# Modulation rows computed once, sent through DRAM and broadcast back, in a two-layer AdaLN attention and expert kernel

## The chip, the core and the metric

The kernel runs on one core of a Trainium2 chip. The metric is the device time of one execution in microseconds (us). The core has a matrix engine (TensorE, PE in the profile; PEld is its weight load), a vector engine (DVE), a scalar engine (ACT), a general engine (POOL) and a queue engine (SP), which here only issues DMAs. They run side by side and wait for each other on semaphores.

## The reference, cut to what matters

The input is x, 16 batches of 256 tokens of 128 features. Two layers follow each other. In each, six vectors per batch are made from a small table c (16 x 128) and a matrix wmod (128 x 768):

```python
mod = (silu(c) @ wmod).reshape(16, 6, 1, 128)
sa, ca, ga, sb, cb, gb = (mod[:, 0], mod[:, 1], mod[:, 2], mod[:, 3], mod[:, 4], mod[:, 5])
```

(sa, ca) shift and scale the normalised input of the attention, and (sb, cb) that of the second block; ga and gb are turned into gates that scale what a block adds to x. Layer 0 has a causal attention of 8 heads with a window of 128, then a second attention of 16 causal heads with a mixture of 8 experts behind it. Layer 1 has a full attention of 16 heads and a routed expert network. All of it is float32.

The kernel forms a gate from a vector g as sign times a clipped size, (g >= 0 ? 0.5 : -0.5) * 2 * max(0.25, |g|), and uses a scale as 1 + c.

## The kernel before

There are three attention stages, called here stage 0 (8 heads, layer 0), stage 1 (16 heads, layer 0) and stage 2 (16 heads, layer 1). The dense expert part lies between stages 1 and 2, the routed one after stage 2. Each stage walks through the 16 batches in a software pipeline. While the heads of batch b are multiplied (function `segment`), the head maxima of batch b+1 are found, the input of batch b+2 is prepared (`prep`), and the output of batch b-1 is finished (`post`). `start` prepares batches 0 and 1 of a stage; the other 14 batches are prepared inside segments.

The order is written out by hand. `order(c)` lists the steps of a segment, and `slots` spreads them over the heads, each step before or behind the value product of its slot. All five engines walk the same table, each taking from a step what is its own, and each engine works strictly in that order. A step on PE writes one of two PSUM banks, `ps_work` or the fourth bank of `ps_four`; `bank_of` gives them out in turn by the step's place among the steps that use PE.

The modulation rows are made anew for each batch and stage, 48 times, in two steps.

- In "stat", DVE copies the batch's column of silu(c) over 128 columns (`c_bcast`, L1449).
- In "mod", PE multiplies it with the wanted columns of wmod (L1665; 128, 384 or 512 columns in stages 0, 1 and 2), which gives the row in all 128 partitions. ACT copies it to `mod` in SBUF (L1290). DVE turns the gate parts into gates by four operations for each part (L1459, L1460, L1464, L1473). POOL adds 1 to the scale part (L1173) in stages 1 and 2.

DVE's next steps stand behind this. "xhat" (L1478) normalises the two token blocks of the batch, and "ht" (PE, L1676) transposes them. DVE also takes the head maxima (L1588 in stages 0 and 1, L1595 in stage 2), for which PE's maximum products (L1767) wait before they reuse one of two PSUM banks.

Lines that the prediction speaks of: `max_scores` L1767 and `exp_scores` L1803 on PE, `pair_values` L1834, "combine" L1725, "rstat" on DVE from L1547, ACT's cast of the selection matrices L1280, PE's small products in the prologue L982, y times the gate L1533, and the loading of the expert weights on SP's queue (`sp_tail`, tile wd).

## Time and profile before

| | us |
|---|---|
| median of 3 runs | 2430.91 |
| lowest and highest | 2418.29, 2470.23 |
| profiled execution, its own time | 2441.24 |
| its span | 2439.4 |
| PE busy (share of the span) | 2040.3 (84%) |
| DVE busy | 1150.1 (47%) |
| ACT busy | 738.2 (30%) |
| POOL busy | 404.9 (17%) |
| mean granted clock of TensorE | 0.713 |

In the rows below a time stamp is us from the start of the span, and L with a number is a line of the kernel. The granted clock is 1.00 at 2.4 GHz and 0.50 at 1.2 GHz, and a value between is a mean over a stretch. A float32 product shows as more than one record ("x2" for one product with 128 stationary columns). In the profile the stages lie at about 22 to 498 (stage 0), 498 to 1300 (stage 1) and 1610 to 2300 us (stage 2). The chain of work that ended last consists of PE to 75%, of DVE to 11%, and of POOL and of unexplained issue time to 5% each.

### The profile page before, as it was taken

The page shows a single profiled execution, that of the slowest core. Times are in us where ns is not written, and L with a number is a line of the kernel's source. Part 1 is how long each engine was busy: PE and PEld are TensorE (multiplying, and loading weights), DVE is VectorE, ACT ScalarE, POOL GpSimd, SP SyncE. Part 2 cuts the span into 40 slices and gives each one's busy share as a digit, 9 for nine tenths or more (in the row PEclk, how much of TensorE's full clock was granted, in tenths as well). Part 3 has the DMA queues.
Part 4 walks back from the last instruction along what each step waited for, and adds up shares of the span by engine and source line. Part 5 has one row for each costly group of instructions (what it writes and reads, how often), then busy time and mean ns, then how long its engine had stood idle before and what let it go on. Part 6 is the DMA issues. An engine that isn't in the chain of part 4 may idle for free.

```text
span 2439.4 us, 35232 instructions
## 1 busy us (share of the span) xinstructions
PE 2040.3 (84%) x11152; PEld 1325.0 (54%) x11152; DVE 1150.1 (47%) x4250; ACT 738.2 (30%) x1580; POOL 404.9 (17%) x643
## 2 busy tenths in 40 slices
PE   5888888968999999899997999968888888898390
PEld 3555555535555555555556888844554555454160
DVE  3454444345344434443426888845544445544202
ACT  1232333213332232233332222213434243434130
POOL 1111111022111211121100000021222122111505
PEclk9887787656555555555557999966878588858595
DMA  6000000000000000000000000010000000000132
GB/s 206 1 1 1 0 0 1 1 0 1 1 1 2 1 1 2 1 1 1 1 1 1 1 0 0 1 35 1 1 1 0 0 0 0 0 1 1 46 105 73
DMA packets 26201, 30.08 MB, mean 12 GB/s; under 512 B 3745, under 2 KB 19393, under 8 KB 25665
## 3 DMA queue, kind: packets, MB, share of 16 engines
q1 hardware_dynamic: 24000, 24.08, 3.1%
q0 software_dynamic: 2048, 4.20, 0.6%
q8 instruction: 68, 1.11, 0.2%
q14 instruction: 85, 0.69, 0.1%
HBM read 19.88 MB, written 8.39 MB: 12 GB/s over the span
## 4 chain that ended last, share of the span: by engine, by line
PE 75%; DVE 11%; POOL 5%; issue 5%; ACT 3%; DMA 1%; SPq 0%; DVEq 0%; POOLq 0%; ACTq 0%
PE ps_out L1834 15%; PE ps_max L1767 8%; PE ps_work L1725 5%; PE ps_four L1803 5%; PE ps_four L1007 5%; PE ps_max L1018 5%; PE ps_four L1681 4%; PE ps_work L1706 3%; PE ps_four L1706 3%; PE ps_four L1686 3%; PE ps_work L1665 2%; PE ps_four L1789 2%; DVE row_max L1595 1%; PE ps_max L1074 1%; DVE ps_max L1588 1%
## 5 line engine op out<-in xcount | busy, mean ns | idle before, releaser
L1401 ACT ACTIVATE attn_f<-ps_four 128x384 f32<-128x384 f32 (+1 forms) x640 | 339.1, 531 | 464.0 <-PE ps_four L1803 463.1
L1834 PE MATMUL ps_out<-attn_f,v_all 128*9 128x256 f32 (+3 forms) x2560 | 418.7, 468 | 0.6 <-ACT attn_f L1391 0.3
L1767 PE MATMUL ps_max<-k_st,q_st 24*128 24x256 f32 (+3 forms) x1280 | 333.9, 417 | 86.4 <-DVE row_max L1595 73.2
L1803 PE MATMUL ps_four<-q_st,k_st 26*128 26x256 f32 (+3 forms) x1280 | 388.2, 392 | 0.0
L1767 PEld LDWEIGHTS ps_max<-k_st,q_st 24*128 24x128 f32 (+1 forms) x1280 | 210.0, 254 | 213.2 <-issue 93.8
L1803 PEld LDWEIGHTS ps_four<-q_st,k_st 26*128 26x128 f32 (+1 forms) x1280 | 262.8, 252 | 31.2 <-issue 21.0
L1588 DVE CUSTOM_DVE_ANT_0 ps_max<-ps_max,q_masks 128x128 f32<-128x128 f32 (+1 forms) x768 | 256.1, 377 | 0.0
L1834 PEld LDWEIGHTS ps_out<-attn_f,v_all 128*9 128x9 f32 (+1 forms) x2560 | 118.4, 108 | 202.6 <-issue 151.6
L1595 DVE TENSOR_REDUCE row_max<-ps_max 128x2 f32<-128x512 f32 x256 | 168.7, 684 | 80.4 <-PE ps_max L1767 79.4
L1789 PE MATMUL ps_four<-masks,ident_bf 128*128 128x128 bf16 x384 | 106.6, 278 | 76.7 <-DVE row_max L1588 59.9
L1725 PEld LDWEIGHTS ps_work<-strips,attn_f 128*128 128x128 f32 x640 | 137.9, 324 | 16.4 <-issue 16.2
L1018 PEld LDWEIGHTS ps_max<-wd,o_both 128*128 128x128 f32 x1024 | 135.0, 193 | 18.3 <-DVE o_both L914 8.0
L1725 PE MATMUL ps_work<-strips,attn_f 128*128 128x36 f32 (+1 forms) x640 | 140.0, 399 | 2.3 <-ACT attn_f L1391 2.3
L1018 PE MATMUL ps_max<-wd,o_both 128*128 128x128 f32 x1024 | 137.1, 277 | 5.7 <-DVE o_both L914 5.5
L1789 PEld LDWEIGHTS ps_four<-masks,ident_bf 128*128 128x128 bf16 x384 | 47.4, 123 | 163.5 <-DVE row_max L1588 59.2
L1581 DVE COPY wait_cell<-one 128x1 f32<-128x1 f32 x384 | 57.1, 149 | 162.4 <-PE ps_max L1767 155.1
L1198 POOL TENSOR_TENSOR split<-rope_ab 128x256 fp32r<-128x256 f32 (+1 forms) x80 | 57.9, 723 | 426.1 <-DVE rope_ab L1504 426.1
L1007 PE MATMUL ps_four<-select,q_st 128*128 128x512 f32 x352 | 119.0, 419 | 1.6 <-DVE select L866 1.6
L1164 POOL TENSOR_TENSOR var_eps<-mean_var,eps 128x2 f32<-128x2 f32 x48 | 9.4, 196 | 646.5 <-DVE mean_var L1452 646.5
L1706 PE MATMUL ps_work<-split,select 128*128 128x256 f32 (+1 forms) x448 | 109.8, 381 | 2.4 <-ACT k_st L1332 2.3
L1791 PE MATMUL ps_four<-masks,ident_bf 128*128 128x128 bf16 x384 | 109.9, 286 | 0.0
L1588 DVE DVE_READ_ACCUMULATOR2_ANT row_max<- 128x1 f32 x768 | 108.0, 141 | 0.0
(243 smaller groups left out, 3069.5 us busy)
## 6 DMA issues: line engine op xcount, KB each, us to landing
wd<-in_L_ffn_W SPq DMA_DIRECT2D x16, 256.0 KB, 2.7
gates_all<-in_select SPq DMA_DIRECT2D x3, 1024.0 KB, 7.3
x_all<-in_L_attn_x SPq DMA_DIRECT2D x8, 256.0 KB, 6.9
slots_dram<-attn_f SPq DMA_DIRECT2D x8, 256.0 KB, 5.5
h_tok<-slots_dram SPq DMA_DIRECT2D x8, 256.0 KB, 2.8
y_dram<-o_both SPq DMA_DIRECT2D x8, 256.0 KB, 2.5
out_x<-x_all SPq DMA_DIRECT2D x16, 128.0 KB
wgu<-in_L_ffn_Wg SPq DMA_DIRECT2D x1, 1024.0 KB, 5.9
```

Source lines behind the costliest of these rows:

```text
L1007: last = nc.tensor.matmul(pairs[pair_of[u]][i], w, x, start=(j == 0), stop=(j == 2))
L1018: last = nc.tensor.matmul(ps_max[:, e % 2, k * D:(k + 1) * D], act_t[:, f, k * P:(k + 1) * P], wd[:, e, f, :], start=(f == 0 and k == 0), ...
L1401: nc.scalar.activation(probs[:, h % 4, 0:w], ps_exp[:, h % 3, 0:w], ACT.Exp, scale=c.scale).then_inc(exp_done, 1)
L1588: ins = nc.vector.tensor_tensor_reduce(ps_max[:, i % 2, first:last], ps_max[:, i % 2, first:last], q_masks[:].rearrange("p n m -> p (n m)" ...
L1595: nc.vector.tensor_reduce(row_max[:, r2, :, h], src, AX_X, ALU.max).then_inc(max_done, 1)
L1706: last = nc.tensor.matmul(bank[:, g * S:(g + 1) * S], select[0:rows, 2 * i + part, 2 * (j % 2) + g, :], split[0:rows, i, part, :], start=( ...
L1725: last = nc.tensor.matmul(columns[:, k, g, i], o_strips[:, g, at:at + P], strips[:, c.kind, 1:1 + w], start=True, stop=True)
L1767: ins = nc.tensor.matmul(bank[:, at:at + keys.stop], q_st[rows, r, g, k * P:(k + 1) * P], k_st[rows, r, g, keys], start=True, stop=True)
L1789: nc.tensor.matmul(bank[:, 0:P], ident_bf[:], masks[:, 0, :], start=True, stop=False, skip_group_check=True)
L1791: nc.tensor.matmul(bank[:, S:S + P], ident_bf[:], masks[:, 0, :], start=False, stop=False, skip_group_check=True)
L1803: ins = nc.tensor.matmul(bank[:, k * S:(k + 1) * S - first], k_st[rows, r, g, k * P:(k + 1) * P], q_st[rows, r, g, first:S], start=not c.c ...
L1834: last = nc.tensor.matmul(ps_out[base:base + c.hd + 1, at + first:at + S], v_tok[c.index][:, r, kb, h // (c.heads // c.kv), :], probs[:, h ...
```

## The change

The rows are computed once for all batches in the prologue. With silu(c) as stationary operand (16 columns) PE multiplies it with four of the six parts of wmod for each layer, ga, sb, cb and gb. ACT copies the result, 16 partitions by 1024, into `mod_rows`. DVE adds 1 to the scales and forms the gates on it at the end of the start of stage 0 (`mod_gates`). SP stores this to a DRAM tensor `mod_dram` and loads the parts that a batch needs, with a broadcast over the 128 partitions, into the ring `mod` of four batches, ahead of time and in the order of the batches; the gates gb of a layer come in one load for all batches. The step "mod" is gone on all engines, and the copy to `c_bcast` with it. In its place "stat" has a tiny copy of eps. DVE waits for the load of a batch's rows where it first uses them, at y in stages 0 and 2 and behind xhat in stage 1. The selection matrices of the next stage are loaded by SP between those loads, as the diff shows.

With one step less the table of slots shifts: almost every step lies half a head or one head earlier, and the two PSUM banks swap roles.

```diff
@@ the table of steps @@
-            return (["stat", "mod", "xhat"] + (["sq", "hn"] if c.index == 1 else []) + ["ht", "combine", "q", "ot"]
+            return (["stat", "xhat"] + (["sq", "hn"] if c.index == 1 else []) + ["ht", "combine", "q", "ot"]
@@ ACT, prologue @@
+            act.wait_ge(pro_pe, 4)
+            nc.scalar.copy(mod_rows.rearrange("b l k d -> b l (k d)"), ps_four[0:NB, 0:2, :]
+                           ).then_inc(mod_rows_out, 1)
@@ DVE, expert part and end @@
+                dve.wait_ge(gates_load, 16)
...
+            dve.wait_ge(gates_load, 32)
@@ PE, prologue @@
+            for layer in range(2):
+                last = nc.tensor.matmul(ps_four[0:NB, layer, :], silu_c[:, layer, :], wmod[:, layer, 2 * D:],
+                                        start=True, stop=True)
+            last.then_inc(pro_pe, 1)
@@ SP @@
+            def load_mod(c, b, r):
+                n = n_of(c, b)
+                if c.index == 1 and not isinstance(b, int):
+                    sp.wait_ge(h_done, b - RING + 1)
+                elif c.index == 2 and not isinstance(b, int):
+                    sp.wait_ge(rt_h, b - RING + 1)
+                elif c.index < 2 and not (c.index == 0 and isinstance(b, int)):
+                    sp.wait_ge(y_out, n - RING + 1)
+                lo, hi = c.parts
+                sp.dma_start(mod[:, r, 0:hi - lo, :],
+                             mod_dram[c.layer, bass.ds(b, 1), lo:hi, :].rearrange("o k d -> (o k) d").partition_broadcast(P)
+                             ).then_inc(mod_load[r], 16)
...
+            sp.wait_ge(mod_rows_dve, 3)
+            sp.dma_start(mod_dram.rearrange("l b k d -> b l k d"), mod_rows).then_inc(mod_store, 16)
+            sp.wait_ge(mod_store, 16)
+            for r in range(RING):
+                load_mod(CFGS[0], r, r)
+            load_select(1)
+            load_later_mods(CFGS[0])
+            for r in range(RING):
+                load_mod(CFGS[1], r, r)
+            load_gates(0)
+            load_later_mods(CFGS[1])
+            sp.wait_ge(moe_done, NB // 2)
+            load_select(2)
+            for r in range(RING):
+                load_mod(CFGS[2], r, r)
+            load_gates(1)
+            load_later_mods(CFGS[2])
             sp_tail(sp)
@@ POOL @@
-                if name == "mod" and c.index > 0:
-                    pool.wait_ge(mod_out, n + 1)
-                    scale = mod[:, r, c.index, :]
-                    nc.gpsimd.tensor_tensor(scale, scale, one[:].to_broadcast([P, D]), ALU.add).then_inc(mod_scale, 1)
@@ ACT @@
-                if name == "mod":
-                    act.wait_ge(mod_mm, n + 1)
-                    at_least(act, y_out, n - RING + 1)
...
-                    nc.scalar.copy(mod[:, r, 0:c.parts, :].rearrange("p a d -> p (a d)"),
-                                   work[bank_of(c, name)][:, 0:c.parts * D]).then_inc(mod_out, 1)
@@ DVE @@
-                    nc.vector.tensor_copy(c_bcast[:, r2, :], silu_c[:, c.layer, bass.ds(b, 1)].to_broadcast([P, P])
-                                          ).then_inc(c_bcast_done, 1)
+                    nc.vector.tensor_copy(var_eps[:, r2, :], eps[:])
...
-                if name == "mod":
-                    dve.wait_ge(mod_out, n + 1)
...
-                        dve.wait_ge(mod_scale, n - NB + 1)
+                        dve.wait_ge(mod_load[r], 4 * (n - r) + 16)
...
+                        dve.wait_ge(mod_load[r], 4 * (n - r) + 16)
                         nc.vector.tensor_tensor(y_tok[:, r2], y, mod[:, r, 0:1, :].to_broadcast([P, BLK, D]),
@@ DVE, called at the end of the start of stage 0 @@
+            def mod_gates():
+                gates = [mod_rows[:, layer, 0::3, :] for layer in range(2)]
+                dve.wait_ge(mod_rows_out, 1)
+                nc.vector.tensor_scalar(mod_rows[:, :, 2, :], mod_rows[:, :, 2, :], 1.0, None, ALU.add)
+                for layer in range(2):
+                    nc.vector.tensor_scalar(gate_rows[:, 0, layer], gates[layer], 0.0, 0.5, ALU.is_ge, ALU.subtract)
+                    last = nc.vector.scalar_tensor_tensor(gate_rows[:, 1, layer], gates[layer], -1.0, gates[layer],
+                                                          ALU.mult, ALU.max)
...
@@ PE @@
-                if name == "mod":
-                    pe.wait_ge(c_bcast_done, n + 1)
-                    nc.tensor.matmul(bank[:, 0:c.parts * D], c_bcast[:, r2, :],
-                                     wmod[:, c.layer, c.mod:c.mod + c.parts * D],
-                                     start=True, stop=True).then_inc(mod_mm, 1)
```

The order moves at three places that matter. The first is PE in the loop of stage 2, from the value product of head slot 1 on (ps_max and ps_four are the maximum and the score products of a head, ps_out the value product). Before:

```order
L1834 MATMUL ps_out<-attn_f,v_all 9x256 x4
L1664 REGISTER_ALU
L1665 MATMUL ps_work<-wmod,c_bcast 128x512
L520 REGISTER_ALU x2
L1767 MATMUL ps_max<-k_st,q_st 128x256
L1803 MATMUL ps_four<-q_st,k_st 128x256
...
L520 REGISTER_ALU
L1676 MATMUL ps_four<-ident,h_tok 128x128 x2
L1824 REGISTER_ALU
L520 ISA
L1834 MATMUL ps_out<-attn_f,v_all 9x256 x4
L1725 MATMUL ps_work<-strips,attn_f 128x36 x8
```

and of the change:

```order
L1857 MATMUL ps_out<-attn_f,v_all 9x256 x4
L517 REGISTER_ALU x2
L1790 MATMUL ps_max<-k_st,q_st 128x256
L1826 MATMUL ps_four<-q_st,k_st 128x256
...
L1699 MATMUL ps_work<-ident,h_tok 128x128 x2
L517 REGISTER_ALU x2
L1803 REGISTER_ALU
...
L1740 ISA
L1748 MATMUL ps_four<-strips,attn_f 128x36 x8
L1847 REGISTER_ALU
L1857 MATMUL ps_out<-attn_f,v_all 9x256 x4
```

The product of 512 columns is gone, the transposes of h_tok stand one head earlier, behind slot 2, and the combine step stands ahead of the value product of slot 3.

The second is DVE at the same place of stage 2. Before:

```order
L1595 TENSOR_REDUCE row_max<-ps_max 128x2
L1459 TENSOR_SCALAR gate_tmp<-mod 128x128
L1460 SCALAR_TENSOR_TENSOR gate_tmp<-mod 128x128
L1459 TENSOR_SCALAR gate_tmp<-mod 128x128
L1460 SCALAR_TENSOR_TENSOR gate_tmp<-mod 128x128
L1464 TENSOR_SCALAR gate_tmp<-gate_tmp 128x128 x2
L1473 TENSOR_TENSOR mod<-gate_tmp 128x128
L1473 ISA
L1473 TENSOR_TENSOR gates_all<-gate_tmp 128x128
L1577 REGISTER_ALU
L1595 TENSOR_REDUCE row_max<-ps_max 128x2
L1478 TENSOR_SCALAR h_tok<-x_all,mean_var,rstd 128x128 x2
```

and of the change:

```order
L1604 TENSOR_REDUCE row_max<-ps_max 128x2
L1487 TENSOR_SCALAR h_tok<-x_all,mean_var,rstd 128x128 x2
L1586 REGISTER_ALU
L1604 TENSOR_REDUCE row_max<-ps_max 128x2
L1586 REGISTER_ALU
```

Between the maxima of slots 1 and 2 DVE now has the two normalisations in place of eight gate operations.

The third is ACT at the very start of the program, of the change:

```order
L648 ACT_TABLE_LOAD
L648 ACTIVATE mod<-ps_work 128x32
L651 COPY ht_all<-ps_four 16x1024
L1321 CAST select<-gates_all 128x2048
L1342 ACTIVATE h_both<-ps_work,mod_t 128x256
```

The copy of the rows stands ahead of the cast of the selection matrices; before, the cast (L1280) followed the first ACTIVATE directly, and the copy of a modulation row (L1290) came behind it.

## Rows read from the trace of the kernel before

**Rows 1.** The page: the chain of work that ended last, share of the span by engine.
```profile
PE 75%; DVE 11%; POOL 5%; issue 5%; ACT 3%; DMA 1%; SPq 0%; DVEq 0%; POOLq 0%; ACTq 0%
```

**Rows 2.** Stretches of stages 0, 1, 2: from:to length, PE busy (instructions), granted clock, DMA, GB/s.
```profile
98.92:425.71 326.79, 274.09 (x1707) 0.78 0.00 1
634.86:1166.89 532.03, 487.86 (x2489) 0.54 0.00 1
1730.23:2177.03 446.80, 383.92 (x2137) 0.76 0.00 0
```

**Rows 3.** Timeline, stage 0, one batch: start, duration, engine, line, out<-in [idle before <-releaser].
```profile
263.13 0.80 PE L1665 MATMUL ps_work<-wmod,c_bcast 128*128 128x128 f32 x2
263.72 0.31 PE L1789 MATMUL ps_four<-masks,ident_bf 128*128 128x128 bf16 x1
266.59 0.45 PE L1676 MATMUL ps_four<-ident,h_tok 128*128 128x128 f32 x1 [1.62 <-DVE h_tok L1478]
...
264.26 0.23 DVE L1459 TENSOR_SCALAR gate_tmp<-mod 128x128 f32<-128x128 f32 x1 [1.08 <-ACT mod L1290]
```

**Rows 4.** Timeline, stage 1, TensorE and VectorE, one batch.
```profile
779.25 1.65 PE L1665 MATMUL ps_work<-wmod,c_bcast 128*128 128x384 f32 x2
780.70 0.31 PE L1789 MATMUL ps_four<-masks,ident_bf 128*128 128x128 bf16 x1
781.32 0.52 PE L1767 MATMUL ps_max<-k_st,q_st 24*128 24x256 f32 x1
783.63 0.28 PE L1789 MATMUL ps_four<-masks,ident_bf 128*128 128x128 bf16 x1 [1.79 <-DVE row_max L1588]
...
781.45 0.23 DVE L1459 TENSOR_SCALAR gate_tmp<-mod 128x128 f32<-128x128 f32 x1 [2.47 <-ACT mod L1290]
```

**Rows 5.** Timeline, stage 2, TensorE and VectorE, one batch.
```profile
2092.96 1.13 PE L1665 MATMUL ps_work<-wmod,c_bcast 128*128 128x512 f32 x2
2094.01 0.38 PE L1767 MATMUL ps_max<-k_st,q_st 24*128 24x256 f32 x1
2097.29 0.38 PE L1767 MATMUL ps_max<-k_st,q_st 24*128 24x256 f32 x1 [2.77 <-DVE row_max L1595]
...
2094.74 0.23 DVE L1459 TENSOR_SCALAR gate_tmp<-mod 128x128 f32<-128x128 f32 x1 [1.21 <-ACT mod L1290]
2096.55 0.68 DVE L1595 TENSOR_REDUCE row_max<-ps_max 128x2 f32<-128x512 f32 x1
2097.15 0.60 DVE L1478 TENSOR_SCALAR h_tok<-x_all,mean_var,rstd 128x128 f32 x2
```

**Rows 6.** Timeline, starts of stage 0 (above) and stage 2 (below).
```profile
17.23 1.90 ACT L1280 CAST select<-gates_all 128x2048 fp32r<-128x2048 f32 x1 [1.92 <-DMA gates_all<-in_select]
17.44 1.89 PE L982 MATMUL ps_work<-silu_c,wmod 128*128 128x16 f32 x8 [0.46 <-DVE dir_mix L752]
24.86 0.69 PE L1676 MATMUL ps_four<-ident,h_tok 128*128 128x128 f32 x2 [1.98 <-DVE h_tok L1478]
...
1611.10 2.05 PE L1665 MATMUL ps_work<-wmod,c_bcast 128*128 128x512 f32 x2 [11.71 <-ACT select L1280]
1616.40 0.66 PE L1676 MATMUL ps_four<-ident,h_tok 128*128 128x128 f32 x2 [3.25 <-DVE h_tok L1478]
```

**Rows 7.** Timeline, stage 2, TensorE, the wait in slot 9.
```profile
2116.10 0.38 PE L1767 MATMUL ps_max<-k_st,q_st 24*128 24x256 f32 x1 [2.16 <-DVE row_max L1595]
```

**Rows 8.** Stretches of stage 2, columns as in group 2.
```profile
2057.20:2067.30 10.10, 10.10 (x44) 0.50 0.00 0
2014.47:2051.64 37.17, 31.22 (x197) 0.86 0.00 0
2051.64:2092.96 41.32, 35.44 (x197) 0.75 0.00 0
```

**Rows 9.** Readers of tile mod (ns min/median/max, first and last start); then DMAs of the page.
```profile
L1533 DVE TENSOR_TENSOR y_tok<-ps_four,mod x16: 412/415/425, 113.9 to 495.7; 128x256 f32<-128x256 f32 x16
...
wd<-in_L_ffn_W SPq DMA_DIRECT2D x16, 256.0 KB, 2.7
```

80 lines of the change are left out of this document (37 added, 43 removed).

## The prediction

> **What bounds the kernel now.** I read the chain of waits first. Three quarters of it are TensorE's own work, 11% are VectorE's [rows 1]. The busy time by stage says the same: TensorE works 274.1 of 326.8 us in stage 0, 487.9 of 532.0 in stage 1 and 383.9 of 446.8 in stage 2 [rows 2]. These stretches run from one "mod" step to another and hold 12, 11 and 11 batches, so a batch takes 27.2, 48.4 and 40.6 us. VectorE, ScalarE and GpSimd have room, and TensorE either works or waits for a result of theirs. A change is thus worth what it takes from TensorE's queue, plus the waits of TensorE that it ends. The timelines show both around the "mod" step. The granted clock comes last: it is 0.78, 0.54 and 0.76 [rows 2], so stage 1 runs nearly all at 1.2 GHz, and the others change between 1.2 and 2.4 GHz.
>
> **What a "mod" step costs in a segment.** Its product takes a place on TensorE. Less plainly, VectorE stands idle until ScalarE has copied the product, then makes gates, and only then takes the next head maximum or normalises the batch, and TensorE waits for that one. The change removes both, so I construct anew the moment at which TensorE gets past the wait.
>
> *Stage 0* [rows 3]. The product starts at 263.13, the masks of the next head at 263.72, so it holds the queue for 0.59 us. The transposes start at 266.59 after a wait of 1.62 for the normalised tokens. VectorE was free at 264.26 - 1.08 = 263.18 and stood until ScalarE's copy. Normalising takes 0.60 [rows 5], and its step now comes ahead of slot 2, so it ends at 263.8, before the heads are through at 264.97 - 0.59 = 264.38. The wait ends. Gain 0.59 + 1.62 = 2.2 us for each batch.
>
> *Stage 1* [rows 4]. The product holds the queue from 779.25 to 780.70, 1.45 us. Slot 3 starts at 783.63 after a wait of 1.79 for a maximum behind the gates. Without them the maximum product of slot 2 ends 1.45 earlier, at 780.39; VectorE, idle since 781.45 - 2.47 = 778.98, has by then nearly finished normalising and scaling (0.60 and, by the 0.41 of an operation of the same size [rows 9], about 1.0 in all). A maximum over two banks' parts takes somewhat more than the 0.68 of stage 2 [rows 5], say 0.9, so slot 3 starts at 781.3. Gain 2.3 us.
>
> *Stage 2* [rows 5]. The product starts at 2092.96, slot 2 at 2094.01, slot 3 at 2097.29 after a wait of 2.77. VectorE is free at 2094.74 - 1.21 = 2093.53, normalises until 2094.13 and ends the maximum of slot 2 at 2094.8. TensorE has by then done slot 2 (until about 2094.0) and the transposes, which come before slot 3 now and took from 2097.89 on about 0.45 [rows 3]. Slot 3 starts at 2094.85, and the transposes no longer follow it. Gain 2.4 + 0.45 = 2.9 us.
>
> A smaller one in stage 2: TensorE waits 2.16 us in slot 9 [rows 7] for a maximum behind "rstat". That step waits for x, which GpSimd updates only after three operations on k. The k step moves half a head ahead and "rstat" stays. I give this 0 to 0.7 us, and take 0.35.
>
> With 14 batches prepared in segments: 14 x 2.2 = 31, 14 x 2.3 = 32, 14 x 3.25 = 45 us, in all 108.
>
> **Starts of the stages.** In stage 2 the product stands from 1611.10 on in the chain that leads to the transposes at 1616.40 [rows 6]. The normalised tokens are ready long before the selection matrices now, so the transposes start at 1611.1: 5.3 us. For batch 1 there, product and gates cost about what a segment's do: 3. In stage 1 I take the same pattern with smaller pieces, 2 + 2. In stage 0 something is added. TensorE's small products end at 19.3; two products of 512 columns follow, each 2.05 by the one at 1611.10, then ScalarE's copy of 1024 columns (half of the 1.90 of the cast of 2048), then that cast, which used to start at 17.23. That makes 19.3 + 4.1 + 0.95 + 1.9 = 26.3, and TensorE waits for the cast, against 24.86: 1.4 us lost. Batch 1 gains about 1.5 back. The gates for all batches are four gate vectors of 128 columns where a batch of stage 2 has two that take 2096.55 - 2094.74 = 1.8 [rows 5], so 3.6 us on VectorE as stage 0's segments begin; TensorE is ahead by two banks and loses 0 to 3.6, I take 2. All starts together: 8.3 + 4 - 1.9 = 10 us gained.
>
> **What is hidden.** The row of batch b is asked for as soon as batch b-4 has released its slot, four batches (over 100 us) ahead; a load of 256 KB lands in 2.7 us [rows 9], and these have 64 to 192 KB. The first is needed at y of batch 0, at 113.9 [rows 9], in the second segment, and the gates are made before the first, a segment of 27 us earlier. SP waits in order behind each slot, and what stands behind it there (the selection matrices of stage 1, the gates gb, the first expert weights of the tail) is needed tens of microseconds later or more. If that cover were gone, VectorE would stand at y, and TensorE two slots later. The copies on ScalarE and the additions on GpSimd were off the path: nothing.
>
> The Trainium skill, DMA: Bandwidth & Descriptors (Anatomy of one DMA), gives a DMA about 2 us of fixed cost, and there are over fifty here; by that, if each were waited for, the sum would shrink by 100 us. The order of the queue says that none is.
>
> **The clock.** In stage 2 a stretch of 10.2 us at 1.2 GHz begins within 2 us after the wait of each of the batches looked at (the first of [rows 8] is one). A batch with one such stretch takes 37.2 us, one with two 41.3 [rows 8], so a stretch costs 4.2. Taking the wait away may end one for each batch, 14 x 4.2 = 59 us, or none, if the clock falls at the next wait instead: the one in slot 9 is followed by a fall only in some batches today. I take 25. For stages 0 and 1 I take nothing: stage 0 falls to 1.2 GHz at the head of a segment before the "mod" step, and stage 1 hardly leaves it.
>
> By the Trainium skill, TensorE: Matmul & The Clock Gate (HAM oscillation), idle gaps between bursts of products throw the clock back; by that rule alone every one of these falls goes, and 59 stands in place of 25.
>
> **Sum.** 108 + 10 + 25 = 143. From the profiled execution's own 2441.2 us that gives 2298. This execution lies 10 above the median of 2430.9 and inside the runs (2418 to 2470), so half of that offset may go too: I say 2295.
>
> **The rivals.**
> 1. *The clock follows fully.* Stage 2 loses all its falls behind "mod" and some of those of slot 9, and stage 1 stays longer at 2.4 GHz. For it: its falls stand right behind a wait that disappears. Against: the trace shows falls elsewhere too. 2441 - 118 - 59 and some 15 for stage 1: about 2250. Chance 0.2.
> 2. *The waits come back.* Only the product's own place on TensorE is gained, 0.59, 1.45 and 1.05 us, as VectorE's next result is late for another reason (combine now comes right behind the transposes, the wait for the squares in stage 1 stands ahead of an exponential). 14 x 3.1 = 43 and 8 for the starts: 2390. For it: TensorE has many short waits of 0.4 to 1 us. Against: VectorE and ScalarE are visibly idle there. Chance 0.07.
> 3. *Slower: the clock falls where the product was.* The place is the head of a segment in stage 2, where a full product of 512 columns goes and small head products, transposes and narrow ones remain. Ten us at 1.2 GHz replace six at 2.4, so a us at 2.4 costs 0.7 more. A batch of stage 2 has about 21 us at 2.4 (clock 0.76); all of it lost is 14 x 15 = 210, against 118 gained: 2533. It decides from a bit over half of that loss on. Against: the busy share of TensorE rises. Chance 0.03.
> 4. *It doesn't do what it says:* VectorE waits for rows at y. If each of 46 batches lost a landing of 2.7, 124 us go and 2298 becomes 2422. Chance 0.03.
>
> The rest, 0.67, is for the forecast. Rival 3 has a rule on its side: the Trainium skill, TensorE: Matmul & The Clock Gate (PE-mode transpose), says that transposes do not count as busy for the clock, and after the change they come right behind the small head products. The trace cannot tell here; by that rule the time is 2533.
>
> **Range and chances.** The upper end lets the segments' gain be a quarter smaller (27) and the clock give nothing (25): 2350, so 2355. The lower one is rival 1's with a little more: 2240. A measurement of this kernel tells about 2% from no change, 49 us, so faster means under 2382. The forecast and rival 1 lie there entirely, rivals 2 and 4 mostly within 2%: 0.89, 0.08, 0.03.
>
> **What would show it.** In the new profile, TensorE's waits of 1.62, 1.79 and 2.77 in slots 2 and 3 are gone, and a batch takes about 25, 46 and 35 us. The first transposes of stage 0 start near 26, those of stage 2 with the end of the cast. No wait of VectorE names the tile mod or its DMA. In stage 2 the granted clock rises above 0.8. I am wrong if waits of the same length stand in front of the transposes or of slot 3, or if the clock of a stage falls by more than 0.05.

## The result: 2196 us, 9.3% under the kernel before, and 100 us under the forecast

The changed kernel took 2196.21 us (median of 4 runs, 2187.74 to 2199.91), the kernel before 2424.6 beside it (2417.49 to 2470.23). The ratio is 0.9067, with a 95% interval of 0.9026 to 0.9108. The forecast was 2295 in a range of 2240 to 2355: the direction was right, and the gain was 228 us where I had 143 (241 between the two profiled executions, which took 2441.2 and 2199.9).

The page of the kernel after: busy shares, then TensorE's busy tenths and granted clock in 40 slices, then the chain of waits by engine.

```profile
PE 1880.1 (86%) x11060; PEld 1242.1 (57%) x11060; DVE 1095.5 (50%) x4002; ACT 728.7 (33%) x1533; POOL 391.0 (18%) x611
...
PE   5889888689989999999979999968898988998390
...
PEclk9998999666565655556559999966887878875595
...
PE 77%; DVE 10%; POOL 5%; issue 5%; ACT 1%; DMA 1%; SPq 0%; DVEq 0%; POOLq 0%; ACTq 0%
```

The chain has hardly changed [rows 1]. The row of the clock has: of its first seven slices, which are stage 0, six read 9 and one reads 8.

To compare kernels I use one pair of marks throughout: from the first transposes ("ht") of the third batch of a stage to those of its sixteenth, 13 batches. The kernel before and then the kernel after in stages 0, 1 and 2 (from:to length, PE busy (instructions), granted clock, DMA share, GB/s):

```profile
71.90:429.20 357.30, 299.39 (x1833) 0.78 0.00 1
560.40:1175.20 614.80, 563.35 (x2911) 0.55 0.00 1
1667.00:2183.10 516.10, 444.58 (x2497) 0.77 0.00 1
```

```profile
69.36:353.10 283.74, 250.26 (x1806) 0.95 0.03 8
455.59:1009.51 553.92, 513.19 (x2884) 0.59 0.01 3
1492.68:1932.10 439.42, 397.70 (x2469) 0.82 0.03 9
```

A batch went from 27.5 to 21.8 us, from 47.3 to 42.6 and from 39.7 to 33.8: 5.7, 4.7 and 5.9 us. The 13 batches of each stage make 211 of the 241 us (14 would make 227). Of the other 30, the starts of the stages, up to their third transposes, gave 15. The end of stage 0, from its last transposes to the first of stage 1, gave 23 (75.9 us at clock 0.59 before, 52.6 at 0.94 after). The rest of the kernel became 8 longer.

How much of it is clock? Two batches of stage 1 of the kernel after do the same work, one all at 1.2 GHz, the other with 20.5 us of it at 2.4:

```profile
568.57:615.93 47.36, 44.95 (x224) 0.50 0.01 4
749.13:784.04 34.91, 31.15 (x224) 0.79 0.02 5
```

The second is 12.45 us shorter and has 47.36 - 14.43 = 32.9 us less at 1.2 GHz: a microsecond there costs 0.38. I take this price for all stages. Other pairs of like batches give between 0.31 (stage 0 before, 25.1 us from 130.41 and 28.0 us from 238.61) and 0.44 (stage 0 after, 20.4 us from 226.66 and 25.0 us from 181.27). From length and clock of the stretches, a batch spent 12.1, 42.6 and 18.3 us at 1.2 GHz before, and 2.2, 34.9 and 12.2 after. The difference, 23.7 us over a batch of each stage, times 0.38 and 14 is **126 us of clock** (53, 41 and 32 by stage); the **101 us** that are left of 227 are products, waits and gates. Both are estimates: by 0.31 to 0.44 the clock's part is 103 to 146. The forecast had 25 and 108, and 10 for the starts.

Where the product and the gates were, TensorE now has this. Stage 0, end of one batch and head of the next:

```profile
220.62 0.50 PE L1879 MATMUL ps_work<-max_t,max_place 128*128 128x256 f32 x2
221.91 0.23 PE L1812 MATMUL ps_four<-masks,ident_bf 128*128 128x128 bf16 x1 [0.78 <-DVE q_st L1618]
223.62 0.23 PE L1812 MATMUL ps_four<-masks,ident_bf 128*128 128x128 bf16 x1 [0.72 <-DVE row_max L1597]
226.66 0.44 PE L1699 MATMUL ps_work<-ident,h_tok 128*128 128x128 f32 x2 [0.81 <-DVE h_tok L1487]
```

Stage 1, then stage 2, the waits of 0.4 us or more around the head of a segment:

```profile
561.13 0.28 PE L1812 MATMUL ps_four<-masks,ident_bf 128*128 128x128 bf16 x1 [1.02 <-DVE row_max L1597]
565.57 0.29 PE L1812 MATMUL ps_four<-masks,ident_bf 128*128 128x128 bf16 x1 [0.90 <-DVE row_max L1597]
568.57 0.69 PE L1699 MATMUL ps_work<-ident,h_both 128*128 128x128 f32 x2 [0.49 <-DVE h_both L1501]
...
1759.47 0.38 PE L1790 MATMUL ps_max<-k_st,q_st 24*128 24x256 f32 x1 [0.85 <-ACT attn_f L1434]
1762.43 0.69 PE L1699 MATMUL ps_work<-ident,h_tok 128*128 128x128 f32 x2 [1.06 <-DVE h_tok L1487]
```

The wait of 1.62 in front of the transposes [rows 3] is 0.81, that of 1.79 in stage 1 [rows 4] is 0.90, and the 2.77 in front of slot 3 of stage 2 [rows 5] is gone, with 1.06 in front of the transposes in its place.

The starts of stage 0 and stage 2, which answer to [rows 6]:

```profile
23.69 1.89 ACT L1321 CAST select<-gates_all 128x2048 fp32r<-128x2048 f32 x1
25.85 0.66 PE L1699 MATMUL ps_work<-ident,h_tok 128*128 128x128 f32 x2 [3.10 <-ACT select L1321]
...
1449.50 0.66 PE L1699 MATMUL ps_work<-ident,h_tok 128*128 128x128 f32 x2 [11.69 <-ACT select L1321]
```

Stage 0 starts 1.0 us later (24.86 before; 1.4 forecast); in stage 2 the transposes follow the cast at once, as forecast. The rows reach VectorE in time: no multiplication of "y" waits for a load. The 16 "mod" loads of stage 2, with their size and the median time to landing in us:

```profile
mod<-mod_dram SPq DMA_DIRECT2D x16, 192.0 KB, 3.2
```

### The profile page after: what moved, and what is told of

Same layout as the page of the kernel before. It is cut to its first block, busy times and chain, and to the rows that moved or that the text cites. A ratio compares the mean times of both kernels' runs of the same rounds, so it can differ in the third digit from the quotient of the medians.

```text
span 2198.1 us, 34707 instructions
## 1 busy us (share of the span) xinstructions
PE 1880.1 (86%) x11060; PEld 1242.1 (57%) x11060; DVE 1095.5 (50%) x4002; ACT 728.7 (33%) x1533; POOL 391.0 (18%) x611
## 4 chain that ended last, share of the span: by engine, by line
PE 77%; DVE 10%; POOL 5%; issue 5%; ACT 1%; DMA 1%; SPq 0%; DVEq 0%; POOLq 0%; ACTq 0%
PE ps_out L1857 14%; PE ps_max L1790 9%; PE ps_four L1748 6%; PE ps_four L1014 5%; PE ps_max L1025 5%; PE ps_four L1826 5%; PE ps_work L1704 4%; PE ps_work L1709 3%; PE ps_four L1729 3%; PE ps_work L1729 3%; PE ps_four L1812 3%; DVE ps_max L1597 2%; DVE row_max L1604 2%; PE ps_max L1081 1%; PE ps_four L1072 1%
## 5 line engine op out<-in xcount | busy, mean ns | idle before, releaser
L1857 PE MATMUL ps_out<-attn_f,v_all 128*9 128x256 f32 (+3 forms) x2560 | 388.4, 440 | 0.3 <-ACT attn_f L1424 0.3
L1826 PE MATMUL ps_four<-q_st,k_st 26*128 26x256 f32 (+3 forms) x1280 | 367.6, 374 | 0.0
L1790 PE MATMUL ps_max<-k_st,q_st 24*128 24x256 f32 (+3 forms) x1280 | 317.2, 404 | 41.3 <-DVE row_max L1604 24.3
L1790 PEld LDWEIGHTS ps_max<-k_st,q_st 24*128 24x128 f32 (+1 forms) x1280 | 198.1, 243 | 154.2 <-issue 73.2
L1826 PEld LDWEIGHTS ps_four<-q_st,k_st 26*128 26x128 f32 (+1 forms) x1280 | 245.7, 237 | 30.2 <-issue 15.5
L1812 PE MATMUL ps_four<-masks,ident_bf 128*128 128x128 bf16 x384 | 101.0, 263 | 70.1 <-DVE row_max L1597 51.5
L1748 PE MATMUL ps_four<-strips,attn_f 128*128 128x36 f32 (+1 forms) x640 | 132.8, 382 | 2.6 <-ACT attn_f L1424 2.3
L1748 PEld LDWEIGHTS ps_four<-strips,attn_f 128*128 128x128 f32 x640 | 127.7, 303 | 10.8 <-issue 10.4
L1812 PEld LDWEIGHTS ps_four<-masks,ident_bf 128*128 128x128 bf16 x384 | 47.3, 123 | 136.2 <-DVE row_max L1597 56.3
L1210 POOL TENSOR_TENSOR var_eps<-mean_var,var_eps 128x2 f32<-128x2 f32 x48 | 9.4, 196 | 583.1 <-DVE mean_var L1482 583.1
L1814 PE MATMUL ps_four<-masks,ident_bf 128*128 128x128 bf16 x384 | 103.5, 270 | 0.0
L1729 PE MATMUL ps_four<-split,select 128*128 128x256 f32 (+1 forms) x448 | 99.5, 354 | 2.4 <-ACT k_st L1365 2.3
```

The lines of the kernel that those rows point to most:

```text
L1729: last = nc.tensor.matmul(bank[:, g * S:(g + 1) * S], select[0:rows, 2 * i + part, 2 * (j % 2) + g, :], split[0:rows, i, part, :], start=( ...
L1748: last = nc.tensor.matmul(columns[:, k, g, i], o_strips[:, g, at:at + P], strips[:, c.kind, 1:1 + w], start=True, stop=True)
L1790: ins = nc.tensor.matmul(bank[:, at:at + keys.stop], q_st[rows, r, g, k * P:(k + 1) * P], k_st[rows, r, g, keys], start=True, stop=True)
L1812: nc.tensor.matmul(bank[:, 0:P], ident_bf[:], masks[:, 0, :], start=True, stop=False, skip_group_check=True)
L1814: nc.tensor.matmul(bank[:, S:S + P], ident_bf[:], masks[:, 0, :], start=False, stop=False, skip_group_check=True)
L1826: ins = nc.tensor.matmul(bank[:, k * S:(k + 1) * S - first], k_st[rows, r, g, k * P:(k + 1) * P], q_st[rows, r, g, first:S], start=not c.c ...
```

## The experiments

The slot of each step is worked out from its place in the list and the list's length. I had written that almost every step moved. Worked out from the list, it is six of 17 in stage 0 (xhat 2 to 1.5, combine 2.5 to 2, and k, qd, y and sel2 by half a head), 13 of 22 in stage 1 and 10 of 20 in stage 2, all by half a head but ht of stage 2, which went from 3 to 2. So the change is three things: gates off VectorE, the product off TensorE, and a shifted table. Each experiment was timed in turn with the kernel before. Times are medians; the ratio to the kernel before has its 95% interval. The kernel before had medians from 2424.6 to 2447.9 beside them, so the difference of two runs' times can be some 20 us off, and the ratios are the safer comparison.

### The three parts one by one

**e1_gate_ops_back**: eight operations of the size of the gates', ahead of xhat on VectorE, with no reader.

```diff
                 if name == "xhat":
+                    for g in range(2):
+                        nc.vector.tensor_scalar(gate_tmp[:, g, 0, :], wq[:, 0, 0, :], 0.0, 0.5, ALU.is_ge, ALU.subtract)
...
                     dve.wait_ge(rstd_done, n + 1)
```

> The changed kernel with eight idle operations of the size of the gate operations (128 x 128, about 1.8 us) put back on VectorE ahead of each normalisation; no product, no copy, nothing else. Theory A (the gain, the clock's part included, comes from ending TensorE's wait behind the gate work): the waits of TensorE at the head of a segment come back, stage 0 falls back to alternating between the two clock levels, a batch there takes 24 to 28 us instead of 20.4, and the whole takes 2330 to 2400 us. Rival B (the clock rose because the full product itself is gone, or because the steps moved in the table): only the delay itself comes back, at most 42 x 1.8 = 76 us, the clock of stage 0 stays above 0.9, and the whole takes 2200 to 2275 us.

Measured: 2246.73, ratio 0.9244 (0.9168 to 0.9321). The gates' time is worth some 50 us, most of it in stage 0, where a batch takes 24.6 us at clock 0.85 against 21.8 at 0.95 and the wait in front of the transposes is 1.61 again; the batches of stages 1 and 2 are 0.3 and 0.7 us longer. The time is in rival B's range, but not the clock of stage 0, which was to stay above 0.9.

**e2_product_back**: a product of 128, 384 and 512 columns at the place of xhat, with no reader.

```diff
+                        if name == "xhat" and True:
+                            at_least(pe, *free[bank_of(c, "ht")])
+                            nc.tensor.matmul(work[bank_of(c, "ht")][:, 0:(128, 384, 512)[c.index]], ident,
+                                             wmod[:, c.layer, 0:(128, 384, 512)[c.index]], start=True, stop=True)
```

> The changed kernel with the float32 product of 128, 384 or 512 columns put back on TensorE where a batch is normalised (identity as stationary operand, nobody reads it); VectorE, ScalarE and GpSimd have none of the old work. Theory A (waits): only the place of the product comes back, 14 x (0.4 + 1.4 + 1.05) = 40 us and a little at the starts, part of it hidden in the wait for the normalised tokens; 2200 to 2245 us, clock of stage 0 above 0.9. Rival B (the product's absence lets the clock stay up): stage 0 alternates again, 2300 us or more.

Measured: 2117.26, ratio 0.8686 (0.8606 to 0.8766). **More work, 79 us less time.** The batches of stages 1 and 2 take 39.9 and 31.6 us at clock 0.68 and 0.92 (42.6 and 33.8 at 0.59 and 0.82 without). Neither expectation had this. In the changed kernel the product's absence is no gain; it costs clock in stages 1 and 2. But e2 doesn't put back all that hung on the old product: it waits for no `c_bcast`, and neither ScalarE's copy nor the gates and the normalised tokens wait for it.

**e3_old_table**: the changed kernel with an empty "mod" in the list, so that every step has its old slot.

```diff
-        PREP = ["stat", "xhat", "sq", "hn", "ht", "q", "k", "qd", "v", "sel0", "sel1", "sel2", "sel3"]
+        PREP = ["stat", "mod", "xhat", "sq", "hn", "ht", "q", "k", "qd", "v", "sel0", "sel1", "sel2", "sel3"]
...
-            return (["stat", "xhat"] + (["sq", "hn"] if c.index == 1 else []) + ["ht", "combine", "q", "ot"]
+            return (["stat", "mod", "xhat"] + (["sq", "hn"] if c.index == 1 else []) + ["ht", "combine", "q", "ot"]
...
-        NO_PE = ["stat", "xhat", "sq", "hn", "rstat", "rmul"]
+        NO_PE = ["stat", "mod", "xhat", "sq", "hn", "rstat", "rmul"]
```

> The changed kernel with an empty step where the old step stood, so that all steps lie in the slots that they had before; the two PSUM banks stay as in the changed kernel and no work is added. Theory A: within 40 us of the changed kernel, 2180 to 2240. Theory C (the shift of the steps by half a head carries much of the gain): 2270 or more, and the clock of stage 0 below 0.85.

Measured: 2350.97, ratio 0.9663 (0.9584 to 0.9742). Without product and gates, but with the old slots, only 82 us of the gain are there. Its three stretches:

```profile
72.30:409.80 337.50, 283.49 (x1806) 0.81 0.02 6
533.90:1115.90 582.00, 541.38 (x2884) 0.55 0.01 3
1597.70:2078.20 480.50, 434.91 (x2470) 0.74 0.03 8
```

The clock stands about where it was before, 0.81, 0.55 and 0.74 against 0.78, 0.55 and 0.77, although the waits are shorter: in stage 1 the 1.79 is 0.90 here too. The head of a segment of stage 0:

```profile
225.14 0.23 PE L1812 MATMUL ps_four<-masks,ident_bf 128*128 128x128 bf16 x1 [0.78 <-DVE q_st L1618]
226.86 0.23 PE L1812 MATMUL ps_four<-masks,ident_bf 128*128 128x128 bf16 x1 [0.72 <-DVE row_max L1597]
230.90 0.69 PE L1699 MATMUL ps_work<-ident,h_tok 128*128 128x128 f32 x2 [1.35 <-DVE h_tok L1487]
```

The first two waits are the same 0.78 and 0.72 as in the changed kernel, and yet here 2.4 GHz ends right behind them, at 228.28, while there it goes on:

```profile
211.21:228.28 17.07, 14.62 (x116) 1.00 0.01 4
228.28:235.10 6.82, 5.47 (x26) 0.50 0.00 0
```

```profile
206.24:266.00 59.76, 51.98 (x398) 1.00 0.02 4
```

**e5b_before_new_slots**, the counterpart: the kernel before, product and gates and all, with the new slots.

```diff
-            names = order(c)
+            names = [n for n in order(c) if n != "mod"]
...
+                if name == "xhat" and with_prep:
+                    table[at // 2][1 + at % 2].append("mod")
```

> The kernel before, with product, copy and gates of the mod step kept, but every other step in the slot where the change has it: xhat at 1.5 instead of 2, combine at 2 (stage 0) and 3 (stage 2), and so on, with the mod step right ahead of xhat. Theory C (the shift of the steps by half a head, which spreads TensorE's waits, carries about 150 of the 240 us): about 2290, 2250 to 2330. Rival A (what counts is that product and gates are gone; with them in place the normalised tokens come late wherever their slot is): 2400 to 2450.

Measured: 2281.16, ratio 0.938 (0.9309 to 0.9452), 150 us less than the kernel before.

```profile
70.70:397.50 326.80, 287.76 (x1833) 0.87 0.00 1
526.10:1050.90 524.80, 457.78 (x2911) 0.72 0.01 1
1543.00:2026.90 483.90, 422.75 (x2494) 0.82 0.00 1
```

With the old slots the removals gain 82 us, with the new ones 85 (2281 to 2196); the shift gains 155 on one side and 150 on the other. By the ratios the removals are worth 3.4% and 3.1% and the shift 6.0% and 6.2% of the time before, and the whole 9.3%. Each side of a pair has the same PSUM banks, so the shift is alone in it; the removals hold all else that differs (product, copy, gates, additions, the loads and the swap of the banks).

Stage by stage the two don't add up: in stage 1 this kernel has clock 0.72 and 40.4 us a batch, and taking product and gates away makes it **2.2 us longer** at 0.59 (one profile each; e17 shows how far stage 1 can move by itself). Nor do e1 and e2 add up to the 85 us: the gates put back cost 50, the product put back gained 79. What is left, the chain from the product over ScalarE's copy to the gates and the swap of the banks, no run puts back by itself.

By the rows of e3, with 0.38 for each microsecond at 1.2 GHz, the 95 us that the removals bring in the stretches at the old slots are, by this estimate, 19 of clock and 76 of work and waits; the 132 that the shift adds are 107 of clock and 25 of waits.

**e4_gates_later**: the kernel before with the gates' operations moved from the "mod" step to the q step on VectorE.

```diff
-                if name == "mod":
-
-                    dve.wait_ge(mod_out, n + 1)
-                    for g, part in enumerate(c.gates):
...
+                if name == "q":
+
+                    dve.wait_ge(mod_out, n + 1)
+                    for g, part in enumerate(c.gates):
...
```

> The kernel before, with one thing moved: VectorE makes the gates of a batch at its step q, some heads later, instead of ahead of the normalisation. Product, copy, additions, number of operations and all else stay. Theory A: the waits of 1.62, 1.79 and 2.77 us end, most of the gain is there without any DRAM: 2424 less about 85 for the waits and about as much for the clock, 2240 to 2300 us. Rival B: 2424 less 85 at most, 2335 to 2400, and the clock of stage 0 stays at 0.75 to 0.80.

Measured: 2416.15, ratio 0.9908 (0.9857 to 0.9958). The kernel gains 22 us by the ratio, and both expectations had more. The waits answer in part: 1.62 [rows 3] is 1.44 in front of the transposes of stage 0, 1.79 [rows 4] is 0.89, and 2.77 [rows 5] is 0.78 in front of slot 3 of stage 2, but a new one of 2.83 stands later in that segment.

### Which steps of the table

**e6b_old_slots_new_xhat** and **e9_first_steps_new**: the table of e3 with xhat, then with xhat, ht and combine, at the new slots.

```diff
+                if name == "xhat":                      # e6b
+                    at = 3
...
+                new = [n for n in names if n != "mod"]  # e9
+                if name in ("xhat", "ht", "combine"):
+                    i = new.index(name)
+                    at = (1, 3, 4)[i] if i < 3 else 2 + i * (2 * c.heads - 2) // len(new)
```

> The changed kernel with all steps in the slots of the kernel before except the normalising (xhat), which stays half a head earlier. The all-old table took 2351, the changed kernel 2196. Theory C1 (the wait of 1.35 us in front of the transposes, which comes back with the old slot of xhat, is what costs, by itself and by the clock): 2190 to 2240. Rival C2 (the places of TensorE's own steps count: combine, q, ot, k and what follows half a head later): 2310 to 2355, as xhat gives back its wait alone, 28 x 0.5 us.

> The changed kernel with the old slots for all steps but the first three behind the head of the segment (xhat, the transposes ht, and combine), which stay where the change has them. All old took 2351, xhat alone new 2321, all new 2196. Theory F (what counts is the stretch of small head products between the last placing product of a batch and the first full products of the next; it gets shorter by the early combine and transposes, and the clock no longer falls in it): 2200 to 2245, granted clock of stage 0 over 0.92. Rival (every step's place counts a little, each by its own waits): 2280 to 2310.

Measured: 2321.49 (0.9535, 0.9459 to 0.9611) and 2300.31 (0.9462, 0.9394 to 0.953). Of the 155 us, xhat alone gives 30, and the first three steps give 51. In stage 0 the wait of 1.35 in front of the transposes is gone in both, and the clock is 0.85 and 0.81, so that wait does not decide. Stage 0 of e9:

```profile
68.40:390.60 322.20, 284.35 (x1806) 0.81 0.02 7
```

**e13_k_qd_old** and **e14_first_steps_old**: the changed kernel with only k and qd, or only xhat, ht and combine, at the old slots.

```diff
+                if name in ("k", "qd"):                 # e13
+                if name in ("xhat", "ht", "combine"):   # e14
+                    old = names[:1] + ["mod"] + names[1:]
+                    i = old.index(name)
+                    at = (1, 3, 4)[i] if i < 3 else 2 + i * (2 * c.heads - 2) // len(old)
```

> The changed kernel with k (all stages) and qd (stage 0) alone at their old slots, half a head later. With these and all later steps old, stage 0 took 24.8 us a batch at clock 0.81 against 21.8 at 0.95, and TensorE had two waits more a batch, 0.48 us for the split halves of the directions and 0.46 for ScalarE's copy of the keys. Theory G1 (these two waits are what makes stage 0 fall): stage 0 at 24 to 25 us a batch, clock 0.80 to 0.86, the kernel at 2240 to 2260. Rival G2 (sel2 and y, half a head later, leave the end of the batch fuller and the head of the next emptier): stage 0 at 22 to 22.8, 2200 to 2215.

> The changed kernel with xhat, ht and combine alone at their old slots. The other way round these three gained 51 us. If the shift of each step has its own price: 2196 + 51 = 2247, 2230 to 2265. Rival (either part alone brings TensorE's busy time under what the clock wants in that stretch, so that with one part missing most of the gain goes): 2270 to 2320. Rival (the later steps alone are enough): 2196 to 2215.

Measured: 2286.65 (0.9346, 0.9233 to 0.9458) and **2171.91** (0.8918, 0.8839 to 0.8996). Two steps (in stages 1 and 2 only k) half a head later lose 90 us (2.8% by the ratios): a batch takes 23.7, 43.2 and 36.4 us. Three others at their old slots gain 24 over the change. No range of either expectation held. By stage, e14 is 24.5 us a batch in stage 0 (worse than 21.8), 38.5 in stage 1 and 32.3 in stage 2 (better than 42.6 and 33.8). In stage 0 the early steps alone (e9, 24.8 us) and the later ones alone (e14) each leave out most of the 4.1 us that the shift gives there. The three stretches of e14:

```profile
69.70:388.50 318.80, 276.83 (x1807) 0.84 0.02 7
508.90:1009.70 500.80, 458.22 (x2885) 0.68 0.01 4
1479.20:1898.60 419.40, 381.23 (x2471) 0.86 0.03 9
```

### Feeding the clock

**e7b_product_stage1**: the added product in stage 1 alone (e2's diff under `c.index==1`).

> The changed kernel with one added product of 384 columns for each batch of stage 1 alone, at the place of xhat, that nobody reads. With such a product in all three stages the kernel took 79 us less than the changed one; in its profile stage 1 with the experts behind it is 46 us shorter, stage 2 with the end 33, stage 0 not shorter. Theory D (the clock of each stage answers to that stage's own product): 2150, 2135 to 2165. Rival (the gain is a matter of where the falls of the clock happen to lie, and a change in one stage moves them in all): anything from 2110 to 2200.

Measured: 2144.17 (0.8835, 0.8778 to 0.8892). Stage 1 goes to 39.5 us a batch at clock 0.70; stages 0 and 2 stay within 0.6 us.

**e16_narrow_product_stage1**: the same product, contracting over 16 of the 128 partitions (`ident[0:16, :]` and the same rows of `wmod`).

> As the changed kernel with one added product of 384 columns a batch in stage 1 (2144, stage 1 at clock 0.70 against 0.59), but the product contracts over 16 partitions, not 128, and so uses an eighth of the array's rows for the same time on TensorE. Theory H1 (any busy time of TensorE counts for the clock): 2144, 2130 to 2160, stage 1 at 0.70. Rival H2 (the used rows of the array count, as the small head products, of 24 to 32 rows, let the clock fall): 2196 to 2220, stage 1 at 0.58 to 0.60.

Measured: 2175.02 (0.889, 0.8809 to 0.8972), stage 1 at 41.6 us and 0.64: between the two, so it settles neither.

**e10_old_slots_product** and **e12_product_first_slot**: a product of 512 columns at the place of stat, in the first slot, with the old table and with the new one.

```diff
+                        if name == "stat":
+                            at_least(pe, *free[bank_of(c, "ht")])
+                            nc.tensor.matmul(work[bank_of(c, "ht")][:, 0:512], ident,
+                                             wmod[:, c.layer, 0:512], start=True, stop=True)
```

> The changed kernel with all steps in the old slots (2351 without more, granted clock 0.81, 0.55 and 0.74 by stage) and one added product of 512 columns a batch that nobody reads, at the place of stat, in the first slot of the segment, amid the small head products. Theory F (that stretch has too little of full products in it): it closes the stretch from inside, stage 0 goes above 0.92 and the kernel gains 46 x 2.5 us or so in spite of the added work: 2230, 2180 to 2270. Rival (the product only costs its own 0.3 to 1.5 us a batch, the fall comes from the waits, which stay): 2360 to 2400.

> The changed kernel with one added product of 512 columns a batch in all stages, at the place of stat in the first slot instead of xhat's (where products of 128, 384 and 512 columns gave 2117). In stage 1 the clock falls 29.5 us behind the transposes, ahead of xhat's place and behind that of stat. Theory F: stage 1's clock over the 0.68 it had with the later product, 2060 to 2105. Rival (the place makes no difference, the sum of full products in the segment counts): 2110 to 2125. Rival (a product ahead of the wait of 1.03 us doesn't help against it): 2196 and up.

Measured: 2295.27 (0.9427, 0.9363 to 0.9491) and 2133.08 (0.8738, 0.8669 to 0.8807). Both lie between the ranges. The product gains 56 and 63 us; in e12 some 47 of it lie in stage 1 (39.3 us at 0.70).

**e8b_unrolled**: the loops over the batches written out. In the changed kernel TensorE stands over 2 us at four jumps back to the head of the loop, not at nine as I had it: twice in stage 0 (2.25 and 2.29, where it waits for VectorE, itself at the jump) and once each in stages 1 and 2 (3.04 and 2.13). In stage 0, then in stage 1:

```profile
266.13 0.23 PE L1812 MATMUL ps_four<-masks,ident_bf 128*128 128x128 bf16 x1 [2.29 <-DVE row_max L1597]
645.02 0.23 PE L1812 MATMUL ps_four<-masks,ident_bf 128*128 128x128 bf16 x1 [3.04 <-issue]
```

```diff
-            with eng.Fori(0, (NB - RING) // RING) as g:
-                for r in range(RING):
-                    segment(c, g * RING + (1 + r), (1 + r) % RING)
-            for b in range(NB - RING + 1, NB):
+            for b in range(1, NB):
```

> The changed kernel with the loop of each stage over its batches written out, so that no engine jumps back every fourth batch (one small VectorE operation of a batch in stage 0 and 1 is left out with it). In the profile of the changed kernel TensorE stands 2.3 us in stage 0 and 3.0 us in stage 1 at these places, and the clock falls behind them, in stage 1 for 112.6 us. Theory E (these waits throw the clock back): nine waits of 2.3 to 3 us go, 20 us, and half the batches of stage 1 take 35 instead of 47 us: 2196 - 20 - 70 = 2105, 2070 to 2140. Rival (the wait costs its own length, and the clock falls all the same): 2170 to 2185. Rival (code that is run once has to be fetched, and TensorE waits for it): over 2196.

Measured: 2184.05 (0.8992, 0.8932 to 0.9052). The rival by which the wait costs its own length had 2170 to 2185. By stage it is less simple. In stage 0 (20.9 us a batch at 0.97) these waits did throw the clock back: in the changed kernel the two falls between 103 and 399 us, at 177.95 and 266.70, come right behind the waits that end at 177.72 and 266.13, and without them TensorE keeps 2.4 GHz for 273 us:

```profile
96.96:370.02 273.06, 239.42 (x1880) 1.00 0.02 5
```

Stage 1, where I expected the gain, has 42.0 us a batch at 0.60 (42.6 at 0.59), and its stretches at 1.2 GHz begin behind a wait of 0.90 as they did behind 3.04.

**e11_unrolled_two_products** (two products of 512 columns in stages 1 and 2, at stat and xhat) and **e15_unrolled_placed_products** (384 columns at xhat in stage 1, two of 512 in stage 2), both unrolled.

> The unrolled version of the changed kernel (2184) with two added products of 512 columns a batch in stages 1 and 2, at the places of stat and of xhat. Theory F: stage 1 goes from 0.60 to 0.80 or more and stage 2 from 0.83 to 0.92: stage 1's batches 37 instead of 42 us, stage 2's 31.5 instead of 33.6, and 2184 - 14 x 5 - 14 x 2.1 = 2085, 2050 to 2110. Rival (one product in slot 1.5 gives all there is): 2105 to 2130. Rival (too much added work): over 2184.

> The unrolled version of the changed kernel (2184) with one added product of 384 columns in stage 1 at the place of xhat (39.5 us a batch against 42.0 so far) and two of 512 in stage 2, at the places of stat and xhat (31.0 against 33.6), none in stage 0 (20.9): each stage in its best form up to now. If the stages' gains stand by themselves: 2184 - 14 x 2.5 - 14 x 2.6 = 2113 less 10 for the starts, 2090 to 2115. Rival (where the clock falls in a stage depends on how it was entered): up to 2140.

Measured: 2134.85 (0.8766, 0.8712 to 0.8821) and 2161.28 (0.8861, 0.8803 to 0.8919). No range held. Stage 2 is short in both (31.0 and 32.1 us). Stage 1 of e15 has e7b's product in it and takes 43.4 at 0.60, against 39.5 at 0.70 in e7b: what a product does there is not fixed by the product.

### Each stage with its own table

**e17_first_old_in_12**: the changed kernel, with xhat, ht and combine at the old slots in stages 1 and 2 only. **e18_first_old_and_product**: the same with e2's product in those stages. Beside e14:

```diff
-                if name in ("xhat", "ht", "combine"):
+                if c.index > 0 and name in ("xhat", "ht", "combine"):
```

> The changed kernel with xhat, ht and combine at their old slots in stages 1 and 2 and at the new ones in stage 0: each stage as it was shortest with whole steps moved (a batch 21.8, 38.5 and 32.3 us, against 21.8, 42.6 and 33.8 of the changed kernel). If the stages stand by themselves: 2196 - 14 x 4.1 - 14 x 1.5 = 2118, 2100 to 2140. Rival (how a stage is entered decides as much as its table): 2140 to 2200.

> The same with one added product a batch that nobody reads, of 384 columns in stage 1 and 512 in stage 2, at the place of xhat. In the changed kernel such products made the batches 39.9 and 31.6 us; here stage 1 and stage 2 start from 38.5 and 32.3. If product and table do the same thing (fill the stretch at the head of the segment), little is left to gain: 2100 to 2130. Rival (they add up): 2050 to 2090. Rival (in these tables the product has nothing to mend and only costs its time, 14 x 2): 2140 to 2170.

Measured: **2099.18** (0.8594, 0.852 to 0.8669) and 2097.89 (0.8605, 0.8555 to 0.8656), each 1 or 2 us under the lower end of its first range. The ratio of e17 is 5.2% under that of the change. The stretches of e17:

```profile
68.90:345.50 276.60, 242.99 (x1807) 0.98 0.03 8
447.80:922.90 475.10, 432.16 (x2884) 0.73 0.02 4
1399.60:1826.70 427.10, 389.17 (x2472) 0.84 0.03 9
```

Stage 1 takes 36.5 us a batch. It has the same table as in e14, where it took 38.5, so a stage with the same instructions can come out 2 us a batch apart. Its batches are still of two kinds, as two of them show:

```profile
512.89:546.97 34.08, 31.33 (x225) 0.80 0.02 6
620.36:667.67 47.31, 44.83 (x224) 0.50 0.02 3
```

The new table makes more of them of the first kind. The product on top changes the total by nothing: stage 2 is shorter (30.3 us a batch at 0.94, from 32.9 at 0.84) and stage 1 longer (39.4 at 0.65, from 36.5 at 0.73). Beside the 2 us between e14 and e17, the 2.9 us of stage 1 can't all be put down to the product.

## Why the prediction was wrong

**What bounds the kernel** was right: TensorE's queue and its waits. The page after says the same.

**Gains in the segments.** I had 2.2, 2.3 and 3.25 us a batch, 108 in all; work and waits came to about 101 by the estimate above. Right in size. In stage 0 the wait did not end, as I wrote, but went from 1.62 to 0.81; in stage 1 it went from 1.79 to 0.90, and in stage 2 a wait of 1.06 stands before the transposes where slot 3 had 2.77. Neither of my two signs of being wrong came, no wait of the same length and no fall of the clock: both looked for a loss only.

**Starts.** 10 forecast, about 15 found. The chain at the start of stage 2 is as I had it. The 23 us at the end of stage 0 I had not looked at.

**What is hidden.** Right: no step waits for a row of mod. The Trainium skill's fixed cost of about 2 us for a DMA (DMA: Bandwidth & Descriptors, Anatomy of one DMA, which is on DMAs issued by GpSimd; these are issued by SyncE), by which 100 us would go if each were waited for, cost nothing here. The loads landed in 2.9 to 3.2 us, and they run batches ahead.

**The clock** is the step that failed: "For stages 0 and 1 I take nothing", and 25 us for stage 2. By the estimate above it gave 53, 41 and 32 us, in all 126. The 25 of stage 2 is near by luck: in e3 the wait of 2.77 in front of slot 3 is down to 0.86 too (at 1778.68), and the clock of stage 2 is 0.74. My reason for stage 0 was that its clock fell before the place of the "mod" step, so that the wait removed came after the fall. The row was read rightly: in the changed kernel, too, the waits of 0.78 and 0.72 stand ahead of that place. But the clock no longer falls behind them. I took the fall for an effect of the wait in front of it alone; e3 and the changed kernel differ in nothing but the places of the steps, and so the fall hangs on these too. For stage 1, "hardly leaves it" was taken as a reason for nothing, while each batch that rises is worth 12.45 us.

**What moved the clock** was in my hands and not costed. The order of the instructions showed steps half a head earlier; I used the shift only to place xhat, the transposes and "rstat". e3 and e5b show that it is worth 150 to 155 of the 228 us. Nothing in the rows of before tells its size: e13 and e14 show steps of the same kind, by the same half head, worth a loss of 90 us and a gain of 24. The way to a right range was to hold, for every stage, the batch that the trace shows at its fastest and slowest clock: stage 0 all at 2.4 GHz is 12.1 x 0.38 = 4.6 us a batch less, 64 us that the lower end left out.

**The rivals.** Rival 1 (the clock follows, 2250) came nearest, but its reason was wrong, and so was its place. The clock did not follow the wait that disappears: with the old slots the removals bring about 19 us of clock. And most of the clock's gain is in stages 0 and 1, where it had 15. Rival 4 fell. Rival 2 fell as a time; of its waits, half came back in stages 0 and 1. Rival 3 (the clock falls where the product was) was given 0.03 and priced for stage 2; its mechanism shows in stage 1: 0.72 with product and new slots, 0.59 without, about 31 us that the change could have had. With an added product in the changed kernel, e2, e7b and e12 have 0.68 to 0.70 there, e15 (unrolled) 0.60. It was outweighed by the shift.

The Trainium skill's rule (TensorE: Matmul & The Clock Gate, HAM oscillation) that idle gaps between bursts throw the clock back agrees only in part. In stage 0 of the changed kernel waits of 2.25 and 2.29 do it. The waits of 0.78 and 0.72, behind which the clock falls in e3, don't do it there, and the jump's 3.04 us in stage 1 does no more than a wait of 0.90. On the Trainium skill's rule on transposes (TensorE: Matmul & The Clock Gate, PE-mode transpose) no run here tells transposes apart.

**Open.** Why half a head matters as it does, in stage 1 above all, why the same instructions of stage 1 take 38.5 us a batch in e14 and 36.5 in e17, and whether the clock answers to TensorE's busy time or to how much of the array is used (e16 lies between), is not settled. That the table's shift is what raised the clock is shown from both sides (e3, e5b). By what it does so, the spacing of the full products or the waits that go with other steps, is not shown.

## What to carry to other kernels

When a step leaves a table from which slots are computed, everything else moves too: put an empty step in its place for one run, and measure removal and shift apart. Where TensorE changes between 1.2 and 2.4 GHz within a batch, bound the clock by the shortest and longest batch with the same work, in every stage, and take neither end for granted. Then try the table stage by stage: three steps put back to their old slots in two stages were worth 97 us here, as much again as the removal of the product and the gates.

## What was not expected of the hardware

A product that nobody reads, one for each batch, made the changed kernel 3.6% faster (2196 to 2117) and its TensorE clock 0.80 instead of 0.76. Batches with the same instructions take 47.4 us or 34 to 35 in one stage of one execution, by whether 2.4 GHz is granted once in them. The same product in a kernel whose stages 1 and 2 had another table gained nothing (2099 and 2098). And from 103 us to the end of stage 0 the changed kernel kept 2.4 GHz through the waits of under 1 us of every batch and lost it only behind the two of 2.25 and 2.29 at the jump back, while with the old slots (e3) it lost it in every batch.
